# Reordered units of a state-space layer, its output projection taken by halves of the tokens, and a feed-forward that begins with one half

## The chip, the cores and the metric

The kernel runs on one core of a Trainium2 chip. The metric is device microseconds of one launch, lower is better.

## What is computed

Two layers on 1024 tokens (4 sequences of 256) of width 512, in fp32, each block followed by a residual sum and a layernorm. The change concerns the second layer:

```
proj = h @ in_proj.T                  # 512 -> gate 8192, xBC 8192+2*8*128, dt 128
xBC  = silu(conv4(xBC))               # depthwise, 4 taps; x, B, C = split(xBC)
cs   = cumsum(dt * A)                 # per head, chunks of 128
Y    = ((C @ B.T) * exp(cs_l - cs_s)) @ (x*dt)  + state terms + x*D
yg   = Y * silu(gate)                 # 8 groups of 1024 channels
out  = (yg * rsqrt(mean(yg**2 per group) + eps) * norm_w) @ out_proj.T
x    = layernorm(x + out)
x    = layernorm(x + ffn(x))          # silu(x@Wg.T*ag) * (x@Wu.T*au) @ Wd.T * ad
```

## The kernel before

Every product of fp32 matrices is made of three TensorE matmuls over a high and a low part (`xh`/`xl`, `wh`/`wl`, `yh`/`yl`): ScalarE rounds the high part, GpSimd (weights) or VectorE (activations) subtracts it for the low one. A matmul here is 128x128 on 512 columns.

`ssm_layer` works on 8 groups of 8 units. The first seven groups are one program loop (`LOOPS`), the last is straight-line code. A unit is one step `j` of 128 gate and 128 X channels for all 1024 tokens. In step `j` TensorE does, in this order: `in_half` for two halves of X of the unit after next in banks 0 and 1 and for two halves of the gate in banks 2 and 3 (48 matmuls, L1718 to L1720), `scan` for four sequences `b` (decayed scores times `xdt`, L1736 and L1738, into banks 0 and 1), then `turn(j+1)`: 8 transpositions of the next X into banks 6 and 7 (L1747). The second halves of the tokens carry the suffix `_1`.

VectorE in step `j`: `skip(j-1,1)` (Y plus D times X, L1541, which frees the Y bank of that half), `times_dt` (L1531, frees the bank of the turn), the gates' silu (L1510), `both(b)` (the two decay products of sequence `b`, L1522, each released by ScalarE's exponentials into banks 4 and 5), three `taps` of the convolution on each half (L1494), `silu` of the halves (L1504), `skip(j,0)`. ScalarE: `exps` (L1252, L1253), `weights_hi` (L1203), `tap` (L1224, the first tap, which writes into one of three X buffers), `tanh` (L1240), squares (L1261). GpSimd: `gate` (L1417), `weights_lo`, `add_square`. The last step of a group works on the B and C tiles of the next group instead of X (`final`), and in the crossing the first X of the next group is made; its `in_half` needs banks 0 and 1, thus `skip(7,0)` and `skip(7,1)`.

The order on each engine is that of the code; engines meet by semaphores, and each waits in order. SP's queue issues, in a step, `load_rows` for b = 0 to 3 (the decay sums of the next unit, each 384 KB; each waits until the exponentials and the scan of its sequence have used the buffer and the unit has been staged), weights (`load_in`), and `stage` (1.5 MB from a table of sums in DRAM to a skewed copy in DRAM, which later row loads read). In the first group each step stages the unit after next; in later groups this is done in every other step.

`project` makes the last group's output: 192 matmuls for 8 tiles of 128 tokens (units by both halves), with one set of mean squares (`ms`, L1792) in front of the second half of unit 0. `o_hi` and `o_lo` split the output weights per unit; VectorE scales and adds into x (L1640). A block ends with a barrier of all engines. `layer1_ffn` then loads and splits its weights (ScalarE L2003, GpSimd L2048), makes the layernorm of 8 tiles on VectorE (L131 to L141), transposes them (L2143), splits `xh`/`xl` (L2096), and runs matmuls (L2133 to L2135) for pairs of feed-forward tiles, each for both halves of the tokens.

## Time and profile before

| | |
|---|---|
| median of 3 runs | 2286.61 us (2282.2 to 2287.29) |
| profiled execution | 2286.95 us, span 2285.1 us |
| TensorE busy, share of the span | 93% |
| VectorE | 68% |
| ScalarE | 52% |
| GpSimd | 36% |
| mean granted TensorE clock | 0.968 |

The profiled execution's time is 1.85 us more than its span. Times in rows count from the span's start. TensorE's "busy" includes pipelined stretches, so idle time and granted clock are what tell more. `<-` ahead of an engine is what ended an idle time.

### The profile page before, as it was taken

How to read it: one execution, taken by the hardware profiler on the slowest of the kernel's cores; microseconds unless marked ns; L12 is line 12 of the kernel's file. 1: busy time of each engine (PE TensorE's matmuls, PEld its weight loads, DVE VectorE, ACT ScalarE, POOL GpSimd, SP SyncE). 2: the span in 40 equal slices, each digit the busy share in tenths (PEclk: the TensorE clock that was granted, in tenths of full speed). 3: DMA queues.
4: the chain of work that ended last, by engine and by line, in shares of the span. 5: the costliest groups of instructions: out<-in, count | busy, mean ns of one | idle time of the engine just before them, and what ended most of it. 6: DMA issues, size and time to landing. Idle time of an engine off the chain costs nothing. (4 is left out here: it accounts for less than half of the span.)

```text
span 2285.1 us, 38143 instructions
## 1 busy us (share of the span) xinstructions
PE 2118.9 (93%) x11176; PEld 1597.7 (70%) x11176; DVE 1556.7 (68%) x3186; ACT 1197.7 (52%) x2846; POOL 830.4 (36%) x680
## 2 busy tenths in 40 slices
PE   6899999997799999999999999999999999987998
PEld 4555555446577877877777787787787777766877
DVE  3666665556588598498488678858848857845345
ACT  4554545413475476377367457647737745742330
POOL 4352524211244245245335325424424532431230
PEclk8799998999899999999999999999999999988999
DMA  6000000003999486688777868768679776702101
GB/s 245 10 1 10 7 1 1 1 0 91 241 232 213 88 232 173 114 230 193 130 189 192 163 159 202 160 112 233 168 125 229 185 139 170 165 22 100 47 10 38
DMA packets 242994, 286.94 MB, mean 126 GB/s; under 512 B 9440, under 2 KB 211424, under 8 KB 242144
## 3 DMA queue, kind: packets, MB, share of 16 engines
q1 hardware_dynamic: 242784, 284.43, 52.5%
q8 instruction: 96, 1.57, 0.3%
q14 instruction: 114, 0.93, 0.1%
HBM read 281.78 MB, written 104.60 MB: 169 GB/s over the span
## 5 line engine op out<-in xcount | busy, mean ns | idle before, releaser
L1718 PE MATMUL b_ps<-xh_keep,wh 128*128 128x512 f32 x1152 | 460.0, 399 | 20.0 <-DVE yt L1541 18.3
L1720 PE MATMUL b_ps<-xh_keep,wl 128*128 128x512 f32 x1152 | 452.1, 392 | 0.0
L1719 PE MATMUL b_ps<-xl_keep,wh 128*128 128x512 f32 x1152 | 451.7, 392 | 0.0
L1405 POOL TENSOR_TENSOR wl<-wraw,wh 128x512 fp32r<-128x512 f32 x144 | 192.8, 1339 | 428.6 <-ACT wh L1203 428.6
L1494 DVE SCALAR_TENSOR_TENSOR xs<-b_ps,par,xs 128x510 f32<-128x510 f32 (+2 forms) x384 | 284.6, 741 | 65.3 <-ACT xs L1224 52.9
L1522 DVE TENSOR_TENSOR decayed<-b_ps,b_scores 128x384 f32<-128x384 f32 x512 | 265.3, 548 | 30.6 <-ACT b_ps L1253 19.9
L1252 ACT ACTIVATE b_ps<-rows,ncs 128x256 f32<-128x256 f32 x512 | 238.3, 465 | 90.5 <-DVE decayed L1522 45.7
L1718 PEld LDWEIGHTS b_ps<-xh_keep,wh 128*128 128x128 f32 x1152 | 218.2, 189 | 66.2 <-DVE yt L1541 16.6
L1720 PEld LDWEIGHTS b_ps<-xh_keep,wl 128*128 128x128 f32 x1152 | 217.9, 189 | 46.7
L1719 PEld LDWEIGHTS b_ps<-xl_keep,wh 128*128 128x128 f32 x1152 | 218.4, 190 | 43.0
L1615 DVE SCALAR_TENSOR_TENSOR yl<-yg,par,yh 128x512 fp32r<-128x512 f32 x128 | 96.1, 751 | 222.0 <-ACT yh L1266 218.3
L1426 POOL TENSOR_TENSOR ssq<-ssq,sq 128x512 f32<-128x512 f32 x112 | 144.4, 1290 | 203.2 <-ACT sq L1261 203.2
L1801 PE MATMUL b_ps<-q_or_out_rounded,yh 128*128 128x512 f32 x512 | 202.4, 395 | 5.0 <-DVE yl L1615 5.0
L1266 ACT ACTIVATE yh<-yg,par 128x512 fp32r<-128x512 f32 x128 | 92.5, 722 | 217.5 <-PE b_ps L1803 217.5
L1802 PE MATMUL b_ps<-q_or_out_rounded,yl 128*128 128x512 f32 x512 | 200.4, 391 | 0.0
L1803 PE MATMUL b_ps<-q_or_out_rounded,yh 128*128 128x512 f32 x512 | 200.3, 391 | 0.0
L1736 PE MATMUL b_ps<-decayed,xdt 128*64 128x256 f32 x1024 | 163.1, 396 | 34.7 <-DVE xs L1494 18.3
L1417 POOL TENSOR_TENSOR yg<-yt,yg 128x512 f32<-128x512 f32 x112 | 162.9, 1455 | 62.2 <-DVE yt L1541 62.2
L1253 ACT ACTIVATE b_ps<-rows,ncs 128x128 f32<-128x128 f32 x512 | 181.8, 355 | 0.0
L596 POOL TENSOR_SCALAR pr<-pr,su 128x256 f32<-128x256 f32 x120 | 112.1, 947 | 151.6 <-DVE su L744 151.6
L1410 POOL TENSOR_TENSOR q_or_out_rounded<-qkv_or_out_weights,q_or_out_rounded 128x512 fp32r<-128x512 f32 x64 | 84.5, 1320 | 220.4 <-ACT q_or_out_rounded L1210 219.9
L1224 ACT ACTIVATE xs<-b_ps,par 128x512 f32<-128x512 f32 x128 | 99.3, 776 | 105.2 <-PE b_ps L1720 105.0
(228 smaller groups left out, 3961.7 us busy)
## 6 DMA issues: line engine op xcount, KB each, us to landing
rows<-skewed_rows SPq DMA_DIRECT2D x256, 384.0 KB, 4.9
skewed_rows<-sum_rows SPq DMA_DIRECT2D x63, 1024.0 KB, 11.6
wraw<-win_dram SPq DMA_DIRECT2D x144, 256.0 KB, 5.5
skewed_rows<-sum_rows SPq DMA_DIRECT2D x63, 512.0 KB, 13.7
qkv_or_out_weights<-wout_dram SPq DMA_DIRECT2D x8, 2048.0 KB, 16.2
w<-w_dram SPq DMA_DIRECT2D x2, 3584.0 KB, 23.3
fraw<-wgu_dram SPq DMA_DIRECT2D x11, 512.0 KB, 3.5
draw<-wd_dram SPq DMA_DIRECT2D x1, 2816.0 KB, 11.7
```

The source lines that it names most:

```text
L1252: nc.scalar.activation(e[:, 0:SEQ], rows[:, b, h, 0:SEQ], ACT.Exp, bias=c0)
L1253: nc.scalar.activation(e[:, SEQ:ROW], rows[:, b, h, SEQ:ROW], ACT.Exp, bias=c1).then_inc(*bk.full(ph, name))
L1405: nc.gpsimd.tensor_tensor(wl[:, n % RING, :], wraw[:, n % RING, :], wh[:, n % RING, :].bitcast(F32), ALU.subtract).then_inc(w_lo.sem, 1)
L1494: ins = nc.vector.scalar_tensor_tensor(y[:, :, back:], z[:, :, 0:SEQ - back], param(g, sub, TAPS - 1 - back), y[:, :, back:], ALU.mult, AL ...
L1522: nc.vector.tensor_tensor(sd[:, b, h, :], ps[bk.bank(ph, name)][:, 0:ROW], sm[:, b, :], ALU.mult)\
L1718: nc.tensor.matmul(out, w_h, x_h, start=(k == 0), stop=False)
L1719: nc.tensor.matmul(out, w_h, x_l, start=False, stop=False)
L1720: last = nc.tensor.matmul(out, w_l, x_h, start=False, stop=(k == KT - 1))
L1736: nc.tensor.matmul(y[h], x[h][0], sd[:, b, h, 0:SEQ], start=True, stop=False)
L1801: nc.tensor.matmul(ps[t][:], y_h, oh[:, j % 2, :], start=(j == 0), stop=False)
L1802: nc.tensor.matmul(ps[t][:], y_l, oh[:, j % 2, :], start=False, stop=False)
L1803: last = nc.tensor.matmul(ps[t][:], y_h, ol[:, j % 2, :], start=False, stop=(j == LAST))
```

## The change

It has three parts.

1. Orders in each group. VectorE's `silu(h[1])` moves ahead of `skip(j,0)`; in the last step `skip(j,0)` moves ahead of the taps of C's first half and `skip(7,1)` between the taps of both halves of C. In step 0 ScalarE makes the weights and the first tap ahead of the first exponentials, and VectorE all taps ahead of `both(0)`. SP issues `stage` behind all four `load_rows`. X has two buffers instead of three, so the first tap waits for the skip of unit `j-1` and not of `j-2`.
2. The last group's end. The projection takes `ENDS`: the second halves of the tokens (tiles 4 to 7, banks 2, 3, 6, 7) of all units, then the first halves. Two of its 16 `end_step` stand ahead of the last step's scans. Output weights are split anew for each half. The upper tiles are added, normalised, transposed and split under the lower half's matmuls. The first two feed-forward weights are loaded in this block.
3. The feed-forward begins with the upper halves of its first two tiles; the lower tiles are normalised under them, then transposed, and the lower halves follow.

Core of the diff:

```diff
-        RING, TXS, XSS = 3, 2, 3
-        wraw = sb("wraw", [P, RING, KT * P])
+        RING, TXS, XSS = 3, 2, 2
+        wraw = raw[:, 0:RING * KT * P].rearrange("p (r c) -> p r c", c=KT * P)
+        fraw = raw[:].rearrange("p (r c) -> p r c", r=2)
...
+        ENDS = [(j, h) for h in (1, 0) for j in range(UNITS)]
+        END_BANKS = [0, 1, 4, 5, 2, 3, 6, 7]
...
-                    load_rows(n + 1, 1)
+                    for b in range(1, BATCH):
+                        load_rows(n + 1, b)
                     if not g:
                         stage(j + 2)
                     elif j % 2 == 0:
                         stage(g * UNITS + 5 + j // 2)
-                    load_rows(n + 1, 2)
-                    load_rows(n + 1, 3)
...
+            sp.wait_ge(*w_lo.made(LOOPS, SUBS - 1))
+            for n in range(2):
+                sp.dma_start(fraw[:, n, :], io["wgu"][n:n + 1].rearrange("a p c -> p (a c)")).then_inc(f_first, 16)
+            sp.wait_ge(f_first, 32)
...
+            def end_hi(ph, g, n):
+                j, h = ENDS[n]
+                if n >= 2:
+                    act.wait_ge(*end_used(ph, n - 2))
+                else:
+                    act.wait_ge(o_loaded.sem, g * 16 + 16)
+                nc.scalar.activation(oh[:, n % 2, :], oraw[:, j, :], ACT.Copy).then_inc(o_hi.sem, 1)
+                if n < 2:
+                    act.wait_ge(*gated.made(ph, f"{j}_{h}"))
+                nc.scalar.activation(yh[:, n % 2, :], yg[:, j, h * HALF:(h + 1) * HALF], ACT.Copy,
+                                     scale=param(g, 2 + j, TAPS + 2)).then_inc(*y_hi.inc())
+            def end(ph, g):
+                for n in range(2, 2 * UNITS):
+                    end_hi(ph, g, n)
+                for t in range(NT // 2, NT):
...
-                    next(e[0])
-                    next(e[0])
+                    if j:
+                        next(e[0])
+                        next(e[0])
                     if more:
                         weights_hi(g, 6 + 2 * j)
                     if h:
-                        tap(ph, gn, h[0], f"Y{j - 2}_0" if j > 1 and not final else None)
+                        tap(ph, gn, h[0], f"Y{j - XSS + 1}_0" if j >= XSS - 1 and not final else None)
+                    if not j:
...
-                    if j == LAST - 2:
+                    if last and LAST - 2 <= j < LAST:
+                        end_hi(ph, g, j - (LAST - 2))
+                    elif j == LAST - 2:
                         out_weights_hi(ph, g, 0)
                         out_hi(ph, g, 0, 1)
-                    if j == LAST - 1:
+                    elif j == LAST - 1:
                         out_hi(ph, g, 0, 0)
...
-                tanh(ph, bc_[3])
                 weights_hi(g, SUBS + 4)
                 tap(ph, g + 1, h[0], f"Y{LAST - 1}_0")
+                tanh(ph, bc_[3])
...
@@ -1461,12 +1507,16 @@
             gate(ph, LAST, 1)
             add_square(ph, LAST, 0)
             add_square(ph, LAST, 1)
-            for j in range(1, UNITS):
-                out_weights_lo(LOOPS, j)
+            for n in range(2, 2 * UNITS):
+                pool.wait_ge(*o_hi.made(LOOPS, n))
+                nc.gpsimd.tensor_tensor(ol[:, n % 2, :], oraw[:, ENDS[n][0], :], oh[:, n % 2, :].bitcast(F32),
+                                        ALU.subtract).then_inc(o_lo.sem, 1)
...
-                        taps(ph, gn, h[0], (1, 2))
+                        taps(ph, gn, h[0])
                         both(0)
-                        taps(ph, gn, h[0], (3,))
-                        both(1)
                         times_dt(ph, g, j, 0)
                         times_dt(ph, g, j, 1)
+                        both(1)
                         both(2)
                     if h:
                         taps(ph, gn, h[1], (1, 2))
                         silu(ph, h[0])
                         taps(ph, gn, h[1], (3,))
                     both(3)
+                    if h:
+                        silu(ph, h[1])
+                    skip(ph, g, j, 0)
                     if h and final:
                         taps(ph, gn, h[2])
-                    skip(ph, g, j, 0)
-                    if h:
-                        silu(ph, h[1])
-                    if h and final:
+                        skip(ph, g, j, 1)
                         taps(ph, gn, h[3])
                         silu(ph, h[2])
-                    if LAST - 2 <= j < LAST:
+                    if last and LAST - 2 <= j < LAST:
+                        end_lo(ph, g, j - (LAST - 2))
+                    elif LAST - 2 <= j < LAST:
                         out_lo(ph, g, 0, LAST - 1 - j)
...
-                skip(ph, g, LAST, 1)
+                taps(ph, g + 1, h[0])
                 silu(ph, bc_[3])
-                taps(ph, g + 1, h[0])
                 taps(ph, g + 1, h[1])
...
+            def end_lo(ph, g, n):
+                j, h = ENDS[n]
+                dve.wait_ge(*y_hi.made(ph, (j, h)))
+                nc.vector.scalar_tensor_tensor(yl[:, n % 2, :], yg[:, j, h * HALF:(h + 1) * HALF], param(g, 2 + j, TAPS + 2),
+                                               yh[:, n % 2, :].bitcast(F32), ALU.mult, ALU.subtract).then_inc(*y_lo.inc())
...
+                for n in range(2, UNITS - 1):
+                    end_lo(ph, g, n)
+                dve.wait_ge(*bk.filled(ph, "ms"))
+                nc.vector.tensor_scalar(rs[:, 1, :], ps[bk.bank(ph, "ms")][:, 0:NT], 0.25 / (UNITS * P), 1.0e-5, ALU.mult, ALU.add)\
+                    .then_inc(*bk.free(ph, "ms"))
+                end_lo(ph, g, UNITS - 1)
+                dve.wait_ge(*bk.drained(ph, "ms"))
+                rsqrt(nc, step, rs[:, 0, :], rs[:, 1, :], rs[:, 2, :])
+                step(nc.vector.tensor_scalar(rs[:, 0, :], rs[:, 0, :], 0.5, None, ALU.mult))
+                end_lo(ph, g, UNITS)
+                end_lo(ph, g, UNITS + 1)
+                for t in tiles:
+                    projected(ph, t)
+                end_lo(ph, g, UNITS + 2)
+                for t in tiles:
+                    dve.wait_ge(*bk.drained(ph, f"o{t}"))
+                    ins = nc.vector.bn_stats(stats(t)[:, 0:6], keep["x"][:, t, :])
+                chain(ins)
+                dve.sem_inc(passed)
+                end_lo(ph, g, UNITS + 3)
+                for t in tiles:
+                    ins = nc.vector.bn_aggr(stats(t)[:, 6:8], stats(t)[:, 0:6])
+                chain(ins)
+                chain(nc.vector.tensor_scalar(upper[:, :, 8], upper[:, :, 7], 1e-5, None, ALU.add))
+                rsqrt(nc, chain, upper[:, :, 9], upper[:, :, 8], upper[:, :, 10])
+                end_lo(ph, g, UNITS + 4)
+                for t in tiles:
+                    nc.vector.tensor_scalar(keep["x"][:, t, :], keep["x"][:, t, :], stats(t)[:, 6:7], stats(t)[:, 9:10],
+                                            ALU.subtract, ALU.mult).then_inc(upper_ready, 1)
+                for n in range(UNITS + 5, 2 * UNITS):
+                    end_lo(ph, g, n)
+                for t in tiles:
+                    cols = slice(t * P, (t + 1) * P)
+                    dve.wait_ge(upper_high, t - NT // 2 + 1)
+                    nc.vector.tensor_tensor(keep["xl"][:, :, cols], ps[END_BANKS[t]][:].rearrange("p (k m) -> p k m", k=KT),
+                                            keep["xh"][:, :, cols].bitcast(F32), ALU.subtract).then_inc(*bk.free(ph, f"xT{t}"))
+                for t in range(NT // 2):
+                    projected(ph, t)
...
+                    if final and last:
+                        end_step(ph, g, 0)
+                        end_step(ph, g, 1)
...
+            def end_step(ph, g, n):
+                j, h = ENDS[n]
+                pe.wait_ge(*o_lo.made(g, n))
+                pe.wait_ge(*y_lo.made(ph, (j, h)))
+                for t in [t for t in (O_TILES if j else O_FIRST) if t // (NT // 2) == h]:
+                    if j == 0:
+                        pe.wait_ge(*bk.freed(ph, f"o{t}"))
+                    c = (t % (NT // 2)) * P
+                    out = ps[END_BANKS[t]][:]
+                    y_h, y_l = (y[:, n % 2, c:c + P] for y in (yh, yl))
+                    nc.tensor.matmul(out, y_h, oh[:, n % 2, :], start=(j == 0), stop=False)
+                    nc.tensor.matmul(out, y_l, oh[:, n % 2, :], start=False, stop=False)
+                    last = nc.tensor.matmul(out, y_h, ol[:, n % 2, :], start=False, stop=(j == LAST))
+                    if j == LAST:
+                        last.then_inc(*bk.full(ph, f"o{t}"))
+                if j < LAST:
+                    last.then_inc(*y_used.inc())
+            def end(ph, g):
+                for n in range(2, 2 * UNITS):
+                    end_step(ph, g, n)
+                    if n == UNITS - 3:
+                        mean_squares(ph)
+                    if n == 2 * UNITS - 3:
+                        for t in range(NT // 2, NT):
+                            pe.wait_ge(upper_ready, t - NT // 2 + 1)
+                            pe.wait_ge(*bk.freed(ph, f"xT{t}"))
+                            out = ps[END_BANKS[t]]
+                            for k in range(KT):
+                                last = nc.tensor.transpose(out[:, k * P:(k + 1) * P], keep["x"][:, t, k * P:(k + 1) * P], cst("ident"))
+                            last.then_inc(*bk.full(ph, f"xT{t}"))
...
+            for e in range(2):
+                gate(ph, 0, e, e, 1, e)
+            for t in LOWER:
+                dve.wait_ge(xh_done, t + 1)
+                nc.vector.tensor_tensor(xl[:, :, t * P:(t + 1) * P], ps[X_BANKS[t]][:].rearrange("p (k m) -> p k m", k=KT),
+                                        xh[:, :, t * P:(t + 1) * P].bitcast(F32), ALU.subtract).then_inc(*bk.free(ph, f"xT{t}"))
...
             ph = Phase("pro", 0, 0)
-            for t in range(NT):
+            for e in range(2):
+                half(ph, 0, e, e, 1)
+            for t in LOWER:
                 pe.wait_ge(normed, t + 1)
                 pe.wait_ge(*bk.freed(ph, f"xT{t}"))
                 for k in range(KT):
-                    last = nc.tensor.transpose(ps[t][:, k * P:(k + 1) * P], x[:, t, k * P:(k + 1) * P], ident)
+                    last = nc.tensor.transpose(ps[X_BANKS[t]][:, k * P:(k + 1) * P], x[:, t, k * P:(k + 1) * P], ident)
                 last.then_inc(*bk.full(ph, f"xT{t}"))
-            for t in range(NT):
+            for t in LOWER:
                 pe.wait_ge(*bk.drained(ph, f"xT{t}"))
-            with nc.Fori(0, PAIRS, engines=bass.OrderedEngineSet([pe.engine]), hint_back_edge=True) as i:
+            for e in range(2):
+                half(ph, 0, e, e, 0)
+            with nc.Fori(0, PAIRS - 1, engines=bass.OrderedEngineSet([pe.engine]), hint_back_edge=True) as i:
                 ph = Phase("loop", i, i)
-                tile(ph, i, 0)
-                tile(ph, i, 1)
```

What stands where, before and after. First VectorE in the last step of a group (`bc` is the tile of B and C, `b_ps0` and `b_ps1` the banks that the next X_0 and X_1 are made in). Before:

```order
L1522 TENSOR_TENSOR decayed<-b_ps5,b_scores 128x384
...
L1494 SCALAR_TENSOR_TENSOR bc<-b_ps2,par,bc 128x2x255
...
L1494 SCALAR_TENSOR_TENSOR bc<-b_ps2,par,bc 128x2x254
...
L1494 SCALAR_TENSOR_TENSOR bc<-b_ps2,par,bc 128x2x253
...
L1541 SCALAR_TENSOR_TENSOR yt<-xs,par,b_ps0 128x512
...
L1504 SCALAR_TENSOR_TENSOR bc<-tx,bc 128x512
...
L1494 SCALAR_TENSOR_TENSOR bc<-b_ps3,par,bc 128x2x255
...
L1504 SCALAR_TENSOR_TENSOR bc<-tx,bc 128x512
...
L1541 SCALAR_TENSOR_TENSOR yt<-xs,par,b_ps1 128x512
```

After:

```order
L1572 TENSOR_TENSOR decayed<-b_ps5,b_scores 128x384
...
L1554 SCALAR_TENSOR_TENSOR bc<-tx,bc 128x512
...
L1591 SCALAR_TENSOR_TENSOR yt<-xs,par,b_ps0 128x512
...
L1544 SCALAR_TENSOR_TENSOR bc<-b_ps2,par,bc 128x2x255
...
L1544 SCALAR_TENSOR_TENSOR bc<-b_ps2,par,bc 128x2x254
...
L1544 SCALAR_TENSOR_TENSOR bc<-b_ps2,par,bc 128x2x253
...
L1591 SCALAR_TENSOR_TENSOR yt<-xs,par,b_ps1 128x512
...
L1544 SCALAR_TENSOR_TENSOR bc<-b_ps3,par,bc 128x2x255
```

Both skips (`yt`) have moved ahead of three taps, and the silu ahead of the first skip.

SP's queue in a step of the first group, before:

```order
L1142 DMA rows<-skewed_rows 128x2x384
L1100 DMA wraw<-win_dram 128x512
L1142 DMA rows<-skewed_rows 128x2x384
L1126 DMA skewed_rows<-sum_rows 128x8x256
L1126 DMA skewed_rows<-sum_rows 128x8x128
L1142 DMA rows<-skewed_rows 128x2x384 x2
```

After:

```order
L1154 DMA rows<-skewed_rows 128x2x384
L1112 DMA raw_weights<-win_dram 128x512
L1154 DMA rows<-skewed_rows 128x2x384 x3
L1138 DMA skewed_rows<-sum_rows 128x8x256
L1138 DMA skewed_rows<-sum_rows 128x8x128
```

The two staging copies stand behind the last two row loads.

TensorE in the last step of the last group (`q_or_out_rounded` is the output weights' high and low part), before:

```order
L1747 MATMUL b_ps7<-consts,xs 128x128 x4
L1736 MATMUL b_ps0<-decayed,xdt 64x256 x2
L1738 MATMUL b_ps0<-decayed,xdt 64x128 x2
...
L1738 MATMUL b_ps1<-decayed,xdt 64x128 x2
L1801 MATMUL b_ps4<-q_or_out_rounded,yh 128x512
L1802 MATMUL b_ps4<-q_or_out_rounded,yl 128x512
```

After:

```order
L1865 MATMUL b_ps7<-consts,xs 128x128 x4
L1944 MATMUL b_ps2<-q_or_out_rounded,yh 128x512
L1945 MATMUL b_ps2<-q_or_out_rounded,yl 128x512
L1946 MATMUL b_ps2<-q_or_out_rounded,yh 128x512
...
L1946 MATMUL b_ps7<-q_or_out_rounded,yh 128x512
L1854 MATMUL b_ps0<-decayed,xdt 64x256 x2
```

24 matmuls of the projection, into banks 2, 3, 6 and 7, stand between the last turn and the last scans.

## Rows read from the trace of the kernel before

**Rows 1.** Header of the profile's page.

```profile
span 2285.1 us, 38143 instructions
```

**Rows 2.** Windows: length, busy (count) of PE, PEld, DVE, ACT, POOL, clock, DMA, GB/s.

```profile
926.00:1112.00 186.00, 179.77 (x976) 144.58 (x975) 141.75 (x231) 113.01 (x243) 75.59 (x56) 0.99 0.75 173
...
2029.00:2073.00 44.00, 44.00 (x181) 35.58 (x180) 17.18 (x32) 12.53 (x19) 8.03 (x6) 0.93 0.00 0
...
716.50:721.00 4.50, 4.44 (x12) 3.49 (x13) 4.43 (x8) 1.17 (x3) 0.34 (x1) 0.62 1.13 151
```

**Rows 3.** TensorE's timeline, steady step: start, length, line, operation, [idle before it].

```profile
808.37 1.09 PE L1747 MATMUL b_ps<-consts,xs 128*128 128x128 f32 x8 [0.26 <-DVE xs L1504]
...
822.73 0.39 PE L1738 MATMUL b_ps<-decayed,xdt 128*64 128x128 f32 x4
...
823.38 1.09 PE L1747 MATMUL b_ps<-consts,xs 128*128 128x128 f32 x8 [0.26 <-DVE xs L1504]
```

**Rows 4.** VectorE's timeline of the same step.

```profile
808.23 0.74 DVE L1541 SCALAR_TENSOR_TENSOR yt<-xs,par,b_ps 128x512 f32<-128x512 f32 x1
...
820.78 1.00 DVE L1522 TENSOR_TENSOR decayed<-b_ps,b_scores 128x384 f32<-128x384 f32 x2
...
822.64 0.68 DVE L1504 SCALAR_TENSOR_TENSOR xs<-tx,xs 128x512 f32<-128x512 f32 x1
```

**Rows 5.** ScalarE's timeline of the same step.

```profile
812.46 0.78 ACT L1224 ACTIVATE xs<-b_ps,par 128x512 f32<-128x512 f32 x1 [0.23 <-PE b_ps L1720]
...
820.88 0.63 ACT L1240 ACTIVATE tx<-xs 128x512 f32<-128x512 f32 x1 [0.70 <-DVE xs L1494]
```

**Rows 6.** TensorE's timeline, end of a group.

```profile
885.38 1.09 PE L1747 MATMUL b_ps<-consts,xs 128*128 128x128 f32 x8 [0.65 <-DVE xs L1504]
...
902.83 0.50 PE L1718 MATMUL b_ps<-xh_keep,wh 128*128 128x512 f32 x1 [2.13 <-DVE yt L1541]
...
907.00 0.47 PE L1718 MATMUL b_ps<-xh_keep,wh 128*128 128x512 f32 x1 [1.13 <-DVE yt L1541]
```

**Rows 7.** VectorE's timeline, end of the same group.

```profile
886.60 0.75 DVE L1615 SCALAR_TENSOR_TENSOR yl<-yg,par,yh 128x512 fp32r<-128x512 f32 x1 [1.28 <-ACT yh L1266]
...
898.67 1.01 DVE L1522 TENSOR_TENSOR decayed<-b_ps,b_scores 128x384 f32<-128x384 f32 x2
...
902.04 0.73 DVE L1541 SCALAR_TENSOR_TENSOR yt<-xs,par,b_ps 128x512 f32<-128x512 f32 x1
```

**Rows 8.** Waits, 560 to 760: waiting tile, releaser, total us, times, longest.

```profile
ACT b_ps L1252 <- DMA rows<-skewed_rows: 24.7, 6, 11.4
```

**Rows 9.** TensorE's timeline in the first group.

```profile
614.11 1.12 PE L1736 MATMUL b_ps<-decayed,xdt 128*64 128x256 f32 x4 [7.04 <-DVE xs L1494]
```

**Rows 10.** SP's queue in the first group.

```profile
642.17 0.36 SPq L1142 DMA_DIRECT2D rows<-skewed_rows  x1
...
658.37 0.36 SPq L1142 DMA_DIRECT2D rows<-skewed_rows  x1
```

**Rows 11.** Tile `rows`, 560 to 740: its loads, issue to landing.

```profile
DMA to landing us min/median/max: 3.1/8.8/15.3
```

**Rows 12.** TensorE's timeline, last step to feed-forward.

```profile
2014.51 1.12 PE L1736 MATMUL b_ps<-decayed,xdt 128*64 128x256 f32 x4 [5.00 <-DVE decayed L1522]
...
2026.73 2.33 PE L1792 MATMUL b_ps<-consts,ssq 128*128 128x1 f32 x16 [3.23 <-issue]
...
2093.50 0.79 PE L2133 MATMUL c_ps<-xh_keep,fh 128*128 128x512 f32 x1 [2.59 <-DVE xl_keep L2096]
```

**Rows 13.** VectorE's timeline over the same stretch.

```profile
2012.16 1.27 DVE L1510 SCALAR_TENSOR_TENSOR yg<-tx,b_ps 128x512 f32<-128x512 f32 x2
...
2074.86 4.85 DVE L131 BATCH_NORM_STATS2 c_stats<-x_keep 128x6 f32<-128x512 f32 x8 [0.33 <-PEq L988]
```

**Rows 14.** ScalarE and GpSimd at the feed-forward's start.

```profile
2078.82 1.06 ACT L2003 ACTIVATE fh<-fraw 128x1024 fp32r<-128x1024 f32 x1 [3.12 <-DMA fraw<-wgu_dram]
...
2079.95 2.34 POOL L2048 TENSOR_TENSOR fl<-fraw,fh 128x1024 fp32r<-128x1024 f32 x1 [5.03 <-ACT fh L2003]
```

More of the change, by code:

```diff
@@ L1781, in steps, with mean_squares @@
                         turn(ph, j + 1)
+            def mean_squares(ph):
+                pe.wait_ge(*sq_added.made(ph, (LAST, 1)))
+                pe.wait_ge(*bk.freed(ph, "ms"))
+                for t in range(NT):
+                    last = nc.tensor.matmul(ps[bk.bank(ph, "ms")][:, t:t + 1], ssq[:, t * P:(t + 1) * P],
+                                            cst("ones")[:, 0:1], start=True, stop=True)
+                last.then_inc(*bk.full(ph, "ms"))
             def project(ph, g):
@@ L2102, in _ @@
+            for e in range(2):
+                gate(ph, 0, e, e, 0, e)
+                low(ph, 0, e, e, 0, e)
+            dve.wait_ge(loaded, 32)
+            with nc.Fori(0, PAIRS - 1, engines=bass.OrderedEngineSet([dve.engine]), hint_back_edge=True) as i:
                 ph = Phase("loop", i, i)
-                tile(ph, i, 0)
-                tile(ph, i, 1)
+                tile(ph, i, 2, 0)
+                tile(ph, i, 3, 1)
             ph = Phase("epi", 0, PAIRS)
-            tile(ph, PAIRS, 0)
+            tile(ph, PAIRS, 0, 0)
```

258 lines of the change are left out of this document (156 added, 102 removed).

## The prediction

> **What bounds the kernel now.** I read the page's header and the windows first. A group of the loop lasts 186.0 us and TensorE is busy in 179.77 of them at a granted clock of 0.99, VectorE in 141.75, ScalarE in 113.01, GpSimd in 75.59 [rows 2]. So TensorE bounds the 2285.1 us [rows 1]. "Busy" counts pipelined matmuls to modelled ends, so I read the gaps in the timeline instead: a steady step goes from one transposition of X (turn) to the next, 808.37 to 823.38, 15.01 us [rows 3]. What a change of order can win is the idle time in front of TensorE's rows, and the half-speed clock that follows a long one.
>
> The gap in a steady step is at the turn. The last scan matmuls began at 822.73 and end by the model at 823.12; a modelled end of 0.39 lies about 0.17 behind the point at which a next matmul can start (in a run each takes 0.227), so the turn could begin at 822.95. It begins at 823.38, and its releaser is VectorE's silu of X_1 [rows 3]. VectorE ended `both(3)` at 821.78, and the silu was issued behind `skip(j,0)`, at 822.64 [rows 4]; its input, ScalarE's tanh, was there at 821.51 [rows 5]. The skip in front of it is needed by nobody so early: its bank is filled again after the turn.
>
> At a group's end there are three gaps. Step 6's turn waited 0.65; `in_half(X0_0)` of the next group waited 2.13 for `skip(7,0)`, and X0_1 1.13 for `skip(7,1)` [rows 6]. VectorE had put the taps of the first half of C ahead of `skip(7,0)`: its last decay product was issued at 898.67 and ended at 899.68, the skip came at 902.04 [rows 7], and the 2.4 us between are those taps. Where these two waits come close together, the clock falls too: 12 matmuls there took 4.50 us at a granted 0.62 [rows 2], where 12 at full clock take 12 x 0.227 = 2.72 (48 of them are the 10.9 us used below; 192 are the projection's 44.0-us window, at 0.93 [rows 2]).
>
> The first group is another regime. ScalarE waited for rows of the decay sums 6 times, 24.7 us in all [rows 8], and TensorE 7.04 us at 614.11 [rows 9]; row loads follow each other every 16.2 us (642.17, 658.37) [rows 10], over the 15.01 of a steady step. The loads take 3.1 to 15.3 us to land, 8.8 in the middle [rows 11].
>
> The end: TensorE idles 5.00 us before the last step's scans, 3.23 before the mean squares [rows 12], and between the end of the projection (window end 2073) and the first feed-forward matmul at 2093.50 TensorE does only the transpositions of the new x [rows 12].
>
> **Term 1, groups 1 to 6.** (a) `silu(h[1])` ahead of `skip(j,0)`. In five turns per group the wait shrinks by 823.38 - 822.95 = 0.43 (bound: it can't start before the scan ends plus issue); a sixth I take at 0.36 since its ScalarE input is a little later; step 6's wait of 0.65 goes whole. 5 x 0.43 + 0.36 + 0.65 = 3.2. The skip then runs 0.68 later, up to 823.3, and frees its bank while the turn (1.09 us) runs: hidden. (b) `skip(7,0)` straight behind silu: both(3) ends at 899.68, silu and skip add 0.62 + 0.66, so the bank is free at 900.95 instead of 902.77: -1.85 of the 2.13. (c) `skip(7,1)` between the C taps: free near 900.95 + 2.3 + 0.7 = 904.0, before TensorE needs it (905.9): the second wait, 1.13, goes, and in the groups that fall to half speed, the 1.7 us of 4.50 - 2.72 there. Average over groups 1.6. (d) At j = 0 weights and tap come before the first exponentials and taps before `both(0)`: one decay product is later by the third tap, about 0.7 us in front of a scan that had slack; I charge 0.2. Sum -3.2 - 1.85 - 1.6 + 0.2 = -6.4 per group, x 6 = **-38.5**. Bounds: at least -20 (turns give half, the clock nothing), at most -45.
>
> (e) X buffers 3 to 2: the tap of X_{j+1} now waits for `skip(j-1,·)`. The later of these skips ran at 808.23 to 808.97 [rows 4], the first tap at 812.46 [rows 5]: 3.5 us of cover, less the 0.7 by which (a) delays the skip. Cost nothing.
>
> **Term 2, group 0.** SP's queue puts the two staging copies (1.5 MB) behind all four row loads. The chain is: row load 3 may be issued when its scan is done, staging follows, its landing releases row load 0 of the next step. Before, staging went out behind load 1, beside loads 2 and 3. Now it starts later by these two loads and must land with nothing to hide it. Against the 16.2 us I estimate a cycle of 17.5: 3.1 for the last landing [rows 11] less about 1.6 that the rows save by not sharing with staging. Seven cycles cost up to 9 us. In return the first row loads are no longer behind staging: the waits of 7.04 [rows 9] and most of a like one before it vanish, some 15 us, of which about 2 stay. Net **-4**, from +8 (the waits stay in another place) to -10. The Trainium skill bears on this place (DMA: Bandwidth & Descriptors, section "Anatomy of one DMA — SWDGE (gpsimd) path"): a DMA has a fixed part of about 2.0 us, mostly the receipt of the last write, worst towards HBM, and the staging writes to HBM. The shortest landing here, 3.1 us, agrees that there is such a part. By that page each of seven cycles, now serial, would cost 2.0, 14 us in all; that would turn -4 into about +1. My term goes by the rows above.
>
> **Term 3, the last group's steps.** Seven turns as in (a), no crossing: **-2.9**.
>
> **Term 4, the end.** Before, the last turn ended at 2014.51 - 5.00 = 2009.51 [rows 12] and the block just ahead of 2074.86, where VectorE begins the next [rows 13]. After: `end_step(0)` starts when bank 2 is free, after silu G7_0, 2012.16 + 1.27 = 2013.4 [rows 13], so 3.9 of the 5.00 us stay; 24 matmuls, 5.4; the scans 5.0; 2023.9. Now `end_step(2)` waits: gates, squares and their sums on GpSimd stand in front of the next weights' low part, and they need the last scan. Before, they were done at 2026.73 [rows 12]; with scans later by 3.4 they end at about 2030, and the step starts at 2030.5. Then 14 steps of 2.72 (38.1), mean squares 2.33 [rows 12], 16 transpositions, 2 x 1.09 [rows 3], and 2.5 for places where VectorE, with layernorm between the `end_lo`, hands its operand over late (it has some 34 us of work under 22 of matmuls and 20 behind; bounds 0 and 6). 2075.6, with 1.8 to the block's end as before: 2077.4, **+2.5**.
>
> Feed-forward: before, 18.7 us from the block's end to the first matmul (2074.8 to 2093.50). The first weights were loaded there (ScalarE waited 3.12), rounded in 1.06, the low part in 2.34 [rows 14], all hidden under the layernorm of 8 tiles that VectorE begins at 2074.86 [rows 13]. Now they are on chip: 1.06 + 2.34 + 0.25 = 3.65 to the first matmul. 48 matmuls of the upper half, 10.9, with 1.4 lost to a slow clock after the gap, hide the lower half's layernorm (about 8 us, half of 4.85 and its like), then 16 transpositions 2.0 and 1.6 until the last low part is written. The point at which these 48 are done and the other half can go on comes 19.6 us after the block's begin; before it came 18.7 + 10.9 = 29.6. **-10.0**. Together -7.5, from -2 to -12.
>
> The Trainium skill (TensorE: Matmul & The Clock Gate, section "HAM oscillation — how this bites in real kernels") says that an idle stretch is paid again as half-speed matmuls behind it. The row of 0.62 [rows 2] agrees. By it the new idle before `end_step(2)` would cost more than its length, some 1.5 us as after the crossing; a result of 2235.5 instead.
>
> **Sum.** -38.5 - 4 - 2.9 - 7.5 = -52.9, from the profiled 2286.95: **2234.0**. The median of the runs shown is 0.34 lower, so the forecast stays at 2234.
>
> **Rivals.** *VectorE becomes the bound of a step.* In the steady step it has only short gaps. If the turn comes earlier and the step is then held by its decay products, half of the loop's gain goes: +19, **2253**. For it: the step-6 stretch, where VectorE waited 1.28 us for yh at 886.60 [rows 7] and then ran without a gap. Against: 141.75 of 186.0 busy. 0.13.
>
> *Group 0's chain is longer.* Staging is the last in each cycle and nothing overlaps it: +8 instead of -4, **2246**. For it: 16.2 us are all transfer. 0.08.
>
> *The end gives nothing.* VectorE delays every step of the second half by a microsecond, and the new idle stays: **2242**. 0.07.
>
> *Slower.* The tap of X_{j+1} waits for the freed buffer. It decides once `skip(j-1,1)` is later than the tap by more than 0.95 us in each of 56 steps (53 us). ScalarE is in order, so behind the tap stand the exponentials and so the scans. At 1.3 us each +73: **2307**. Against: 3.5 us of cover, so the skip would have to move by 4.5. 0.04.
>
> *The change doesn't do what it says*: TensorE's waits move to the next bank, within 0.2%: **2284**. 0.02. A difference under 0.2% (4.6 us) can't be told from none here.
>
> **Chances and range.** The forecast holds 0.66, own range 2222 to 2244. With the VectorE and group-0 cases it reaches to 2254; the low end is nearly the sum of the favourable bounds (-45, -10, -2.9, -12: 2217), 2218. Faster 0.94, same 0.02, slower 0.04.
>
> **What would show it.** The windows of groups 1 to 6 are 179 to 180 us long, not 186. The turn's releaser is PE's own scan. At X0_0 the wait is under 0.4 and the clock in the crossing stays at 1. In group 0 the row loads follow each other every 17.5 us with no wait over 3 us at the start. At the end, a gap of about 4 us, then one of 6 to 7 behind the scans, and the first feed-forward matmul 3.7 us behind the barrier. Wrong it would be if ScalarE's taps of X wait for a skip, if VectorE's share of a step is whole, or if the new end is longer than the old by more than 12 us.

## The result and the profile after

The changed kernel takes 2265.68 us (median of 4 runs, 2263.59 to 2266.57) beside 2285.04 (4 runs) of the kernel before: ratio 0.9915, 95% interval 0.9897 to 0.9932. It is 19.4 us faster where 52.9 were forecast, and outside the range. The profiled execution has a span of 2263.8 us, 21.3 less than [rows 1].

The rows below are those of the changed kernel that answer to the ones before; its `turn` is L1865. First windows, with the columns of [rows 2]: one group, from turn 1 to the next group's turn 1, and the stretch behind the wait in the new end.

```profile
969.39:1153.05 183.66, 179.00 (x978) 143.72 (x977) 144.24 (x233) 112.96 (x243) 72.18 (x56) 1.00 0.76 175
2013.50:2031.50 18.00, 18.00 (x77) 14.58 (x78) 6.74 (x17) 4.98 (x8) 6.76 (x5) 0.88 0.00 0
```

A group lasts 183.7 us, not 186.0 and not 179.6. TensorE's timeline in that group shows where it is lost:

```profile
984.07 1.09 PE L1865 MATMUL b_ps<-consts,xs 128*128 128x128 f32 x8
...
998.92 0.65 PE L1854 MATMUL b_ps<-decayed,xdt 128*64 128x256 f32 x4 [1.38 <-DVE xs L1544]
...
1000.56 1.09 PE L1865 MATMUL b_ps<-consts,xs 128*128 128x128 f32 x8
```

From turn 3 (1000.56) to turn 4 (1015.26) it is 14.70 us, under the 15.01 of [rows 3]; no turn up to this one waits for a silu any more (the one behind step 6 still does, 0.64 us, see below). But from turn 2 (984.07) to turn 3 it is 16.49, and one scan waited 1.38. What it waited for is two engines away. ScalarE's timeline:

```profile
988.43 0.48 ACT L1267 ACTIVATE b_ps<-rows,ncs 128x256 f32<-128x256 f32 x1 [4.40 <-DMA rows<-skewed_rows]
```

The exponentials waited for row loads to land, VectorE's decay products for them, the last scan for VectorE. SP's queue just ahead of it (its rows are marked SPq), first in the changed kernel and then in the kernel before, in the same group:

```profile
966.85 1.25 SPq L1138 DMA_DIRECT2D skewed_rows<-sum_rows  x2
...
970.51 0.89 SPq L1117 DMA_DIRECT2D qkv_or_out_weights<-wout_dram  x1
971.50 5.42 SPq L1154 DMA_DIRECT2D rows<-skewed_rows  x1
```

```profile
972.06 1.25 SPq L1126 DMA_DIRECT2D skewed_rows<-sum_rows  x2
...
978.30 0.85 SPq L1105 DMA_DIRECT2D qkv_or_out_weights<-wout_dram  x1
981.38 1.61 SPq L1142 DMA_DIRECT2D rows<-skewed_rows  x1
```

Turn 1 stands at 969.39 in the one and at 979.43 in the other. So the 1.5 MB of staging went out 7.4 us ahead of turn 1 before and goes out 2.5 us ahead of it now, and the 2 MB of output weights follow 3.7 us behind it in place of 6.2: the burst has moved towards the rows of unit 2. The first of these row loads (971.50 and 981.38 above) takes 16.6 us to land, where it took 13.6.

The end of a group, and the end of the layer, on TensorE:

```profile
877.06 1.09 PE L1865 MATMUL b_ps<-consts,xs 128*128 128x128 f32 x8 [0.64 <-DVE xs L1554]
...
891.21 0.65 PE L1854 MATMUL b_ps<-decayed,xdt 128*64 128x256 f32 x4 [0.69 <-DVE bc L1544]
...
893.21 0.50 PE L1836 MATMUL b_ps<-xh_keep,wh 128*128 128x512 f32 x1 [0.29 <-DVE yt L1591]
...
896.40 0.47 PE L1836 MATMUL b_ps<-xh_keep,wh 128*128 128x512 f32 x1 [0.15 <-DVE yt L1591]
```

```profile
1995.13 0.77 PE L1944 MATMUL b_ps<-q_or_out_rounded,yh 128*128 128x512 f32 x1 [4.49 <-DVE yg L1560]
...
2013.48 0.80 PE L1944 MATMUL b_ps<-q_or_out_rounded,yh 128*128 128x512 f32 x1 [7.26 <-POOL q_or_out_rounded L1512]
...
2066.24 0.79 PE L2326 MATMUL c_ps<-xh_keep,fh 128*128 128x512 f32 x1 [4.63 <-POOL fl L2225]
```

The waits of 2.13 and 1.13 in [rows 6] are 0.29 and 0.15, and a scan ahead of them that waited 0.16 waits 0.69. In the end stand 4.49 and 7.26 where [rows 12] had 5.00 and 3.23. In the last group VectorE stood 6.91 us, and nothing that the trace shows ended this wait ("issue"). The second row is the same instruction in the kernel before, where the wait is 2.65:

```profile
1935.69 1.02 DVE L1572 TENSOR_TENSOR decayed<-b_ps,b_scores 128x384 f32<-128x384 f32 x2 [6.91 <-issue]
```

```profile
1954.64 1.02 DVE L1522 TENSOR_TENSOR decayed<-b_ps,b_scores 128x384 f32<-128x384 f32 x2 [2.65 <-issue]
```

All of it as a sum. Each number is a difference of starts of `turn` rows, and the last is the span less the last turn:

| stretch | before | after | forecast | measured |
|---|---|---|---|---|
| up to the first turn 0 row | 573.03 | 572.82 | 0 | -0.2 |
| first group, turn 0 to 7 | 126.09 | 121.50 | -4 | -4.6 |
| 7 crossings, turn 7 to turn 1 | 658.9 | 646.3 | -19.5 | -12.6 |
| 6 groups, turn 1 to 7 | 553.3 | 549.0 | -19.2 | -4.3 |
| last group, turn 1 to 7 | 97.09 | 99.86 | -2.9 | +2.8 |
| from there to the end | 276.68 | 274.25 | -7.5 | -2.4 |

The forecast's 0.2 for step 0 is in the crossings here. The forecast priced six crossings (3.25 us each), and the measured number is of seven (1.8 each). Its -19.2 is for seven turns per group, one of which lies ahead of turn 1. The second table gives the steps from turn to turn, of the third group and the last, and the mean from turn 2 to 3 over the six loop groups:

| kernel | third group, 1 to 7 | mean 2 to 3 | last group, 1 to 7 |
|---|---|---|---|
| before | 15.03 15.02 15.37 15.02 15.01 16.60 | 15.02 | 17.79 16.56 16.97 14.97 14.98 15.82 |
| after | 14.68 16.49 14.70 14.70 14.70 15.99 | 16.68 | 18.08 14.69 21.36 15.81 14.70 15.22 |

### The profile page after: what moved, and what is told of

It reads as the page before. It is cut to its first block and busy times, and to the rows that moved or that the text cites. A ratio compares the mean times of both kernels' runs of the same rounds, so it can differ in the third digit from the quotient of the medians.

```text
span 2263.8 us, 38171 instructions
## 1 busy us (share of the span) xinstructions
PE 2117.7 (94%) x11176; PEld 1595.2 (70%) x11176; DVE 1583.3 (70%) x3197; ACT 1199.1 (53%) x2854; POOL 815.5 (36%) x688
## 5 line engine op out<-in xcount | busy, mean ns | idle before, releaser
L1449 POOL TENSOR_TENSOR wl<-raw_weights,wh 128x512 fp32r<-128x512 f32 x144 | 187.0, 1299 | 402.3 <-ACT wh L1218 402.3
L1665 DVE SCALAR_TENSOR_TENSOR yl<-yg,par,yh 128x512 fp32r<-128x512 f32 x112 | 90.7, 810 | 180.7 <-ACT yh L1281 177.0
L1925 PE MATMUL b_ps<-q_or_out_rounded,yh 128*128 128x512 f32 x448 | 176.0, 393 | 5.0 <-DVE yl L1665 5.0
L1461 POOL TENSOR_TENSOR yg<-yt,yg 128x512 f32<-128x512 f32 x112 | 145.1, 1296 | 92.3 <-DVE yt L1591 92.3
L1927 PE MATMUL b_ps<-q_or_out_rounded,yh 128*128 128x512 f32 x448 | 174.4, 389 | 0.0
L1926 PE MATMUL b_ps<-q_or_out_rounded,yl 128*128 128x512 f32 x448 | 174.4, 389 | 0.0
L1281 ACT ACTIVATE yh<-yg,par 128x512 fp32r<-128x512 f32 x112 | 80.9, 722 | 174.1 <-PE b_ps L1927 174.1
L1454 POOL TENSOR_TENSOR q_or_out_rounded<-qkv_or_out_weights,q_or_out_rounded 128x512 fp32r<-128x512 f32 x58 | 76.4, 1317 | 194.5 <-ACT q_or_out_rounded L1225 192.7
## 6 DMA issues: line engine op xcount, KB each, us to landing
qkv_or_out_weights<-wout_dram SPq DMA_DIRECT2D x8, 2048.0 KB, 16.5
```

Of the source, the lines that this page charges most:

```text
L1449: nc.gpsimd.tensor_tensor(wl[:, n % RING, :], wraw[:, n % RING, :], wh[:, n % RING, :].bitcast(F32), ALU.subtract).then_inc(w_lo.sem, 1)
L1925: nc.tensor.matmul(ps[t][:], y_h, oh[:, j % 2, :], start=(j == 0), stop=False)
L1926: nc.tensor.matmul(ps[t][:], y_l, oh[:, j % 2, :], start=False, stop=False)
L1927: last = nc.tensor.matmul(ps[t][:], y_h, ol[:, j % 2, :], start=False, stop=(j == LAST))
```

## The experiments

Ratios are to the kernel before on the same chip, with 95% intervals. The stretch ahead of the first turn, in which these kernels do the same, varies from 569.5 to 579.3 us between single traces, so I compare stretches of traces and whole ratios apart. One trace is kept of each kernel, and the stall behind turn 2 varies between traces: over the six loop groups, from turn 1 to 7, the six kernels that have the changed order there (the changed kernel, e5, e6, e7, e10, e12) take 545.3 to 554.5 us. The five with staging in its old place (e1, e2, e8, e9, e13) take 541.3 to 543.4.

**e1, staging back in its place.**

```diff
-                    for b in range(1, BATCH):
-                        load_rows(n + 1, b)
+                    load_rows(n + 1, 1)
                     if not g:
                         stage(j + 2)
...
+                    load_rows(n + 1, 2)
+                    load_rows(n + 1, 3)
```

> The changed kernel with SP's two staging copies put back between row loads 1 and 2, in every group. Theory A (late staging lands together with the 2 MB of output weights and delays the rows of unit 2 of each group): the step that ends with turn 3 falls from a mean of 16.7 to about 14.7 us in the six loop groups (-12), the first group gets its old 16.0 us period back (+4 to +5), together about 2258 us against 2265.7. Theory B (TensorE now comes earlier to rows that land when they always did, whatever the place of the staging): the step stays near 16.5 us and the time is 2268 to 2271. Theory C (two X buffers or the shared weight buffer delay it): as B.

0.9892 (0.9875 to 0.9910). The step from turn 2 to 3 is 14.68 to 14.70 in all six groups; what is left of the stall is 0 to 0.9 us one step earlier and, in three groups, 0.2 to 1.8 from turn 3 to 4. The six groups are 6.3 us shorter than in the changed kernel, the last one 3.6, and the first 7.1 longer. This is theory A, with a smaller price than the 12 us. The ratio's interval overlaps that of the changed kernel, so it is the steps that show it.

**e2, staging late in the first group alone** (`if not g: stage(j + 2)` behind row load 3, the other branch between 1 and 2).

> The changed kernel with staging behind the four row loads in the first group alone, and between row loads 1 and 2 in all others. Theory A: both gains, the first group as in the changed kernel and no stall in the step to turn 3: 2253 us. Theory B and C: no difference to the changed kernel, 2265 to 2267.

0.9872 (0.9858 to 0.9887), which is 0.0043 or 10 us under the changed kernel; these two intervals don't overlap. From turn 2 to 3 it is 14.68 to 14.71 in all six; the first group takes 124.3 us, between 121.5 and e1's 128.6. Theories B and C are out as the whole cause.

**e3, the output weights in step 3** (`if j == 3: load_out(g)`).

> The changed kernel with the 2 MB load of output weights issued in step 3 of a group in place of step 1; they are first read at the end of step 5. Theory A: without that load beside them the rows of unit 2 land in time, the step to turn 3 is 14.7 to 15.0 us, -10 to -12, about 2255 us; some of it may come back as a wait in step 4. Theory B: a volume that is the same in every order: the stall moves to step 4 or 5 and the time stays at 2262 to 2266.

0.9920 (0.9906 to 0.9934), no gain. The time is a miss for the forecast made from theory A, and the trace is the best evidence for it: turn 2 to 3 is 14.70 in all groups, and now turn 4 to 5 is 15.88 to 18.98. ScalarE's wait has moved with the load:

```profile
1018.68 0.48 ACT L1267 ACTIVATE b_ps<-rows,ncs 128x256 f32<-128x256 f32 x1 [3.78 <-DMA rows<-skewed_rows]
```

```profile
997.37 1.25 SPq L1138 DMA_DIRECT2D skewed_rows<-sum_rows  x2
...
1001.07 0.56 SPq L1117 DMA_DIRECT2D qkv_or_out_weights<-wout_dram  x1
```

Step 3 comes behind an even step too, so staging (997.37) is again issued straight ahead of the 2 MB. I had overlooked that.

**e4, late staging alone, in the kernel before.**

> The kernel before with staging behind the four row loads and nothing else changed. Theory A: the first group gains about 4.6 us, the loop groups lose 0.5 to 1.5 us each at the step to turn 3 (TensorE comes later than in the changed kernel, so less), in sum 2280 to 2288 against 2285. Theory B: only the first group changes, 2280.

1.0017 (1.0005 to 1.0029): slower by 4 us, where -5 to +3 was expected. The first group gains 2.9 us, the six groups lose 6.6 (turn 2 to 3 15.4 to 17.6), the last 1.4, and the crossing behind the first group 2.1.

**e5, the new orders alone**, with the old projection and feed-forward.

> The kernel before with the new orders alone (those of all engines in a group, the staging place and two X buffers among them), with the old projection and feed-forward. If the parts add up as the two traces suggest, this carries nearly all of the change: groups -20 to -22, end 0, ratio 0.9915 + 0.001 = 0.9925. If the new end is what the prediction said (-7.5), the ratio here is 0.995.

0.9909 (0.9893 to 0.9925): all of the change's gain, so that the ratios show nothing for the new end, though they leave some 5 us open. From the last turn to the end this trace has 274.93 us, the changed kernel 274.25. The other traces say a little more: four kernels with the old end (before, e4, e5, e10) take 274.9 to 276.7 us there, eight with the new end as it is in the changed kernel take 273.4 to 274.7. The new end is worth about 2 us.

**e6, the first two steps of the new projection behind the last scans.**

```diff
+                    for b in range(BATCH):
+                        scan(ph, j, b)
                     if final and last:
                         end_step(ph, g, 0)
                         end_step(ph, g, 1)
-                    for b in range(BATCH):
-                        scan(ph, j, b)
```

> The changed kernel with the two first steps of the new projection behind the last scans in place of ahead of them. Theory D (they hold up the scans, and with them gates, squares and all that follows, and leave the wait behind the scans uncovered): the wait ahead of the scans is 5.0, that behind the two steps shrinks from 7.3 to about 1.5 us: idle 6.5 in place of 11.8, -5 us, ratio 0.9893. Rival E (the two steps fill a wait that would be there anyway): +2 us.

0.9886 (0.9868 to 0.9904); the end is 269.5 us, 4.75 less. TensorE's timeline and a window behind the scans:

```profile
1991.11 1.12 PE L1854 MATMUL b_ps<-decayed,xdt 128*64 128x256 f32 x4 [6.02 <-DVE decayed L1572]
...
2004.99 0.50 PE L1944 MATMUL b_ps<-q_or_out_rounded,yh 128*128 128x512 f32 x1 [2.15 <-POOL q_or_out_rounded L1512]
```

```profile
1997.00:2015.00 18.00, 15.83 (x70) 12.35 (x68) 5.33 (x5) 7.26 (x12) 11.94 (x10) 1.00 0.01 1
```

TensorE idles 8.2 us in these two waits in place of 11.8, and behind the shorter one the granted clock stays at 1.00 (2.4 GHz), where it was 0.88. Behind the wait of 6.02 it does fall (0.71 from 1991 to 1997), but there under scans, three of which wait for VectorE anyway (0.15, 0.35, 0.68). This is theory D. The two intervals of the ratios overlap by a little, so the stretch in the trace is the evidence; e9, with the same edit, has 269.9, e13 271.6.

**e7, step 0 ordered as before** (ScalarE: exponentials ahead of weights and tap; VectorE: `both(0)` ahead of the third tap, `both(1)` ahead of `times_dt`).

> The changed kernel with the orders of step 0 on ScalarE and VectorE as they were before. If these cost the 0.58 us that stretch from turn 0 to turn 1 grew by (9.61 to 10.20), seven to eight groups give -4 us; if the growth is paid for by an earlier turn 0, no difference or +2.

0.9861 (0.9841 to 0.9881). The stretch from turn 0 to turn 1 is 9.25 us in place of 10.20, in each of six groups, and turn 7 to turn 0 is as in the changed kernel (82.15 to 82.22 behind all groups but the first). So the new order of step 0 costs 0.95 us a group, over 6 us in all; the ratio fell by 0.0054, 12 us, and the rest is within what the two intervals leave open.

**e8, the output weights in four parts**, on e2 (`if 1 <= j <= 4: load_out(g, j - 1)`, 512 KB each).

> The kernel of e2 (staging late in the first group alone) with the 2 MB of output weights loaded as four parts of 512 KB in steps 1 to 4. Theory A, that a burst of transfers delays the rows: the steps left at 15.0 to 15.6 us in place of 14.70 fall to 14.7 to 14.8, -4 to -6 us against e2, about 0.985. If what is left comes from the volume and not the burst, no change against e2 (0.987).

0.9849 (0.9829 to 0.9870), but not as expected. The six groups are 0.9 us longer than in e2 (604.6 against 603.7), with waits of 0.5 to 2.2 us at other steps; only the last group is shorter, 104.1 against 108.6. By this pair of traces the size of the burst no longer matters in the loop once staging is in its old place.

**e9, combined**: e8, e7 and e6 together.

> The changed kernel with what the runs have favoured so far, together: output weights in four parts, staging late in the first group alone, step 0 ordered as before, the first two steps of the new projection behind the last scans. If the gains of e8 (0.0066), e7 (0.0054) and e6 (0.0029) against the changed kernel's 0.9915 add up: 0.9766, about 2232 us. If those of e7 and e8 come from the same wait (both reach it at steps 1 to 2), 0.981.

0.9835 (0.9815 to 0.9854), 2252.78 us. The gains don't add up. The six groups sum to 596.8 us from turn 0 on, which is e8's 604.6 less the 0.95 of e7 six times and 2.1 more, and the end to 269.9, so those parts are there; the ratio shows less, and this trace has 579.3 us ahead of the first turn, 6.5 more than the changed kernel. Why that stretch varies stays open.

**e10, three X buffers**, on e5 (`XSS = 3`).

> The kernel of e5 (new orders alone) with three X buffers in place of two. If the tap waits for the skip of unit j-1 nowhere (3.5 us of cover in the rows of before), no difference: 0.991, steps of 14.7. If the slower rival has some part in the shortfall, steps fall under 14.7 or the stall at turn 3 goes, and the ratio falls by over 0.002.

0.9910 (0.9894 to 0.9925), the same as e5. Steps without a stall are 14.68 to 14.70, and the stall behind turn 2 does not go: 16.0 to 18.8 in this trace, 15.6 to 16.6 in e5's. The rival in which two buffers slow the kernel is out.

**e11, `skip(j,0)` ahead of `silu(h[1])` again.**

```diff
+                    skip(ph, g, j, 0)
                     if h:
                         silu(ph, h[1])
-                    skip(ph, g, j, 0)
```

> The changed kernel with skip(j,0) ahead of silu(h[1]) again, at the end of every step. By the prediction's term (0.43 per turn, 0.65 at step 6, and about 0.65 of the wait at the crossing) that is +3.8 us per group and 30 us in all; by the steps of the two traces (15.02 against 14.70, 16.6 against 15.99) +0.32 x 5 + 0.61 + up to 0.65 at the crossing, +2.9 per group, +22 us in all, ratio 1.001.

0.9949 (0.9934 to 0.9964), +0.0034 or 8 us: a third of what I expected. The steps are 15.01 to 15.04 again, as forecast. But the stall behind turn 2 shrinks as TensorE comes later (15.3 to 16.8 in place of 15.6 to 18.6), and turn 7 to turn 0 is 0.55 shorter with the skip first (turn 0 to 1 is 0.36 longer). Six groups from turn 1 to 7: 558.5 against 549.0, 9.5 us where the steps without a stall would give 2.6 each, 15.6. So while rows are late, part of what the silu gains is given back, 6 of the 15.6 us by this pair of traces. Theory B of e1 was right to that extent; as the stall varies between traces, how much it is stays open.

**e12, no staging in the last group**: its three stagings are issued at the end of the group before.

```diff
-                    elif j % 2 == 0:
+                    elif j % 2 == 0 and g < LOOPS:
...
-                    for k in range(1 if g else 2, 5):
+                    for k in range(1 if g else 2, 5 if g < LOOPS - 1 else UNITS):
```

> The changed kernel with the three stagings of the last group issued at the end of the group before (during the crossing), none in the last group. Theory F: the idle times of ScalarE (4.9) and VectorE (6.9) in the last group, which end with no releaser in the trace, come while staging and row loads fill the DMA engines, and with late staging they grew. Without staging there they fall under 2 us, the last group from 109.8 to 103 to 105 us, ratio lower by 0.002 to 0.003 than 0.9915. Rival G: they are fixed costs of straight-line code and stay: no change in the last group; the crossing might lose 1 us.

0.9890 (0.9871 to 0.9909). From the last group's turn 1 to 7 it is 94.8 us in place of 99.9, from turn 3 to 4 15.96 in place of 21.36, and VectorE's idle time is down:

```profile
1937.09 1.02 DVE L1572 TENSOR_TENSOR decayed<-b_ps,b_scores 128x384 f32<-128x384 f32 x2 [1.98 <-issue]
```

The crossing ahead of it is 1.1 longer, as rival G allowed, and ScalarE's wait stays at 3.60. So theory F holds for VectorE's wait, the larger one. The interval of the ratio overlaps that of the changed kernel, but the other traces bear the wait out. It is 2.0 to 2.1 us in the two kernels without staging in the last group (e12, e13), 2.65 to 4.4 in the five with staging in its old place (before, e1, e2, e8, e9), and 5.9 to 8.1 in the eight with late staging; e4, the kernel before with nothing but the late staging, has 6.02. ScalarE's wait shows no such order by the staging: it is 3.2 to 4.9 us in twelve kernels, 2.2 and 2.0 in e8 and e9, and none over 1.5 in e13; what it depends on stays open. That VectorE waits for instructions that arrive late behind the staging is my reading; no row names them.

**e13, e9 with the same move.**

> The kernel of e9 with the same move. By theory F its last group falls from 102.7 to about 100 and the ratio from 0.9835 to about 0.982; by G no change.

0.9804 (0.9788 to 0.9819), 2245.32 us: the best version, some 25 us under the changed kernel by the ratios. Against e9 the gain is less sure: the last group falls from 102.7 to 100.7 as expected, but the crossing ahead of it is 1.9 longer (84.07), and the two intervals overlap.

## Why the prediction was wrong, point by point

Of the 31.6 us that the trace falls short of the forecast, 14.9 are in the six groups, 6.9 in the crossings, 5.7 in the last group and 5.1 in the end.

**Where it failed: "SP's queue puts the two staging copies (1.5 MB) behind all four row loads" was priced in the first group alone.** The change does it in every group, and terms 1 and 3 charged nothing for it. Staging goes out 5 us later in the step, closer to the output weights, and the rows of unit 2 land late: turn 2 to 3 takes 16.68 us instead of 14.70 on average, 12 us in six groups. e1, e2, e3 and e4 show it from four sides. In the traces of the changed kernel and of the six variants that leave staging and output weights where it has them in the loop (e5, e6, e7, e10, e11, e12) this step takes 15.3 to 18.8 us; in the five with staging in its old place it takes 14.7 in every group. The trace of before had the hint: ScalarE already waited for rows at this step, over 1 us in three of the six groups, so there was no cover to lose:

```profile
810.21 0.48 ACT L1252 ACTIVATE b_ps<-rows,ncs 128x256 f32<-128x256 f32 x1 [1.26 <-DMA rows<-skewed_rows]
```

Undone in the loop it is worth 10 us by the ratio (e2), and 6.3 in e1's six groups, not 12: waits of up to 0.9 and 1.8 us came back at the steps beside it. That a TensorE that runs earlier meets other landings is my reading of these.

**(a) silu ahead of the skip.** The mechanism holds: a steady step fell from 15.01 to 14.70 us, and with the skip put back it is 15.01 again (e11). That is 0.31 per turn, not 0.43. The turn begins 0.32 behind the start of the last scan matmuls (983.75 and 984.07), and I had assumed 0.22 (822.73 and 822.95). Step 6 fell by 0.61 where 0.65 was said, but not for the reason given: the wait of 0.65 at its turn was to go whole, and 0.64 still stands, so the gain came from earlier in the step. Outside the stalled steps six turns make -2.75 per group, for the 2.8 or so that the forecast had for six. That this agrees is luck in part: it takes in 0.67 at turn 4, and in two groups a stall of 0.6 and 0.5 at turn 2 of the kernel before, which the forecast did not have.

**(b) and (c), the skips of step 7.** (b) is right, 2.13 to 0.29, -1.84 for a forecast of -1.85. (c) is mis-sized: 1.13 to 0.15 is -0.98, and I had 1.6, an average over groups in which the second wait stands and groups in which the clock falls. All seven crossings of before are alike from turn 7 to turn 0: 84.4 to 84.5 us in the three with the second wait and a clock of 1.00 throughout, 84.6 in the four in which the clock fell to 0.5 behind the first wait and there was no second. So the slow clock took the wait's place and cost 0.2 more, not 1.7. And 0.5 came back as a wait of a scan, 0.69 in place of 0.16 (its releaser is a tap of VectorE).

**(d) step 0.** Charged at 0.2, it costs 0.95 (e7). The stretch grew by 0.6 only (9.61 to 10.20), since the silu gains 0.36 at the turn behind it (9.61 to e7's 9.25). The scan that had no slack was not the first: the first two of step 0 start without a wait, and the third waited 0.62 for VectorE, which does all taps ahead of `both(0)` now and `times_dt` ahead of `both(1)`.

**(e) two X buffers** cost nothing, as forecast (e10).

**Term 2, the first group**: -4.6 measured, -4 forecast. That the two are near is luck in good part. The chain was to cost up to 9 us and the vanished waits to give 13. The first row loads of the steps follow each other every 17.0 us on average, where it was 16.5 before and 17.5 was forecast: 4 us over seven cycles. The waits did not fall to 2 but came to stand elsewhere (4.47 and 3.06, then 3.06 and 2.65), and TensorE's idle time from turn 0 to 7 fell by 6.3 us, 22.2 to 15.9. Nor is one trace sure here: kernels with the late order there take 120.7 to 125.5, the kernel before 126.1 and e1, with the old order there, 128.6. By the fixed 2.0 us of the Trainium skill (DMA: Bandwidth & Descriptors, section "Anatomy of one DMA — SWDGE (gpsimd) path") the term was estimated at +1. The trace doesn't follow that: the chain grew by 0.5 us a cycle. That section is on transfers issued by GpSimd, and these are issued by SP.

**Term 3** was -2.9 and came out at +2.8. Most of it is the step from turn 3 to 4, 16.97 to 21.36, with VectorE's wait of 6.91 for 2.65. It goes by the staging: with staging in its old place the last group is 3.6 us shorter from turn 1 to 7 (e1; 1.2 in e2), with none 5.1 (e12).

**Term 4, the end.** -7.5 forecast, -2.4 in the trace, about 2 by all traces (e5). The order of events was right, and the waits too (4.49 for 3.9, 7.26 for 6.6, 2.4 in VectorE's late operands for 2.5, 3.55 from barrier to the first feed-forward matmul for 3.65). From the last turn to the barrier it takes 6.7 us longer than before, where 2.5 was summed, and from there to the end 9.2 less for 10.0, so it is the new projection that falls short. What was mis-sized is the half-speed clock. Behind the wait of 4.49 the 24 matmuls of the first two steps take 8.3 us at a granted clock of 0.66, where 5.4 were summed; the scans behind them take 2.8 for 5.0, so that little of this is left in the sum. Behind the wait of 7.26 the clock is 0.88 over 18 us, which is 2.2 us lost, and the stretch from 2013.48 to the last matmul of the projection takes 48.1 us where 45.1 were summed. The first 48 feed-forward matmuls take 13.96, for 10.9 + 1.4:

```profile
2066.24:2080.20 13.96, 13.96 (x49) 11.19 (x50) 8.10 (x19) 1.38 (x2) 2.27 (x1) 0.78 0.60 252
```

The Trainium skill (TensorE: Matmul & The Clock Gate, "HAM oscillation — how this bites in real kernels") has this: an idle stretch is paid again at half speed. The trace agrees at three places, with 2.8, 2.2 and 3.1 us. I had 1.4 in the sum for the last of them, and 1.5 for the second kept out of it. e6 is the counter-proof: less idle time, clock 1.00 behind the second wait, -4.75 us. That the two `end_steps` hold up the scans, and with them everything that the third waits for, was in my own sum (the scans later by 3.4), without my asking what they'd give in the other place.

**Rivals.** None came as stated. The one nearest is "half of the loop's gain goes" (2253), for another cause: not VectorE, but a transfer. The end did give little, but by the clock and not by VectorE's operands, which came late by 2.4 as summed. The slower rival is out (e10).

## What to carry to other kernels

An issue that is moved in a queue is to be priced in every phase that runs the same code, and the first question is which other transfer it now meets; a consumer that already waited a microsecond for a load, as ScalarE did here, has no cover left. When one engine is made faster, the load that was just in time can become the bound, and part of the gain stays there until the transfers are moved too. And work put ahead of a chain to fill a wait delays the chain: it belongs behind the last link that something else is waiting for.

## What was not expected of the hardware

VectorE in straight-line code stood still with no releaser in the trace, at the same instruction in all fifteen kernels: 5.9 to 8.1 us with late staging, 2.65 to 4.4 with staging in its old place, 2.0 to 2.1 with none in that group. A single load wait of 4.40 us on ScalarE reached TensorE as a wait of 1.38 us. And the crossing took 84.4 to 84.6 us whether or not TensorE's clock fell in it.
